# State-space stage: residuals of B and C formed by TensorE, two copies on ScalarE, and new instruction lists

## What is computed

```python
x = resid * lax.rsqrt(jnp.mean(resid * resid, -1, keepdims=True) + EPS) * norm_w
skip = x @ skip_w.T
xe = x @ in_w.T                      # then a causal convolution of 4 taps over time
xs = silu(conv(xe) + conv_b)
delta = softplus(xs @ wd1.T @ wd2.T + wd2_b)
A = -exp(A_log)                      # 256 channels x 16 states
Bm, Cm = xs @ wb.T, xs @ wc.T        # 16 values each per position
h = exp(delta * A) * h + (delta * xs) * Bm      # a scan over 256 positions
y = sum over states of h * Cm
y = (y + xs * W_D) * silu(skip)
out = resid + y @ out_w.T
```

## Time and profile before

| | us |
|---|---|
| median of 3 runs | 2874.43 |
| lowest, highest | 2872.92, 2874.45 |
| the profiled execution | 2875.4 |
| its span | 2873.6 |
| state-space stage, START to the end of MF | 0 to about 637 |

### The profile page before, as it was taken

The page is one execution under the profiler, slowest core; times in us unless marked ns, Lnnn a source line. Parts: engine busy times, 40 slices in busy tenths (PEclk is TensorE's granted clock), DMA queues, the critical chain, the costliest instruction groups (busy, mean ns, idle before and its releaser), DMA issues. The chain is left out here.

```text
span 2873.6 us, 55943 instructions
## 1 busy us (share of the span) xinstructions
PE 2647.1 (92%) x18868; PEld 1819.6 (63%) x18868; DVE 2260.1 (79%) x3798; ACT 2225.5 (77%) x6114; POOL 1223.4 (43%) x1089
## 2 busy tenths in 40 slices
PE   6888888789999999999999999997899999999997
PEld 3454445356666666666777777774566666666665
DVE  8999999976767777777689999996667777676774
ACT  5788878557777777777799999995677777777775
POOL 5776777664444444444400000001444444444442
PEclk8999999999999999999999999997999999999998
DMA  3000000000000000000000000000000000000000
GB/s 98 1 1 1 1 1 1 0 1 2 1 1 1 13 13 1 1 1 1 13 14 2 2 2 1 2 1 1 1 2 1 1 2 13 17 5 7 7 7 7
DMA packets 15672, 17.84 MB, mean 6 GB/s; under 512 B 3838, under 2 KB 12863, under 8 KB 15295
## 3 DMA queue, kind: packets, MB, share of 16 engines
q1 hardware_dynamic: 15390, 14.26, 1.7%
HBM read 12.16 MB, written 2.10 MB: 5 GB/s over the span
## 5 line engine op out<-in xcount | busy, mean ns | idle before, releaser
L1064 POOL TENSOR_TENSOR f_p<-f_p,f_rs 128x512 f32<-128x512 f32 (+1 forms) x256 | 321.2, 1255 | 907.4 <-DVE f_rs L1013 907.3
L901 ACT ACTIVATE f_p<-pair,f_nm 128x128 f32<-128x128 f32 (+1 forms) x1024 | 387.4, 392 | 125.2 <-DVE f_nm L1002 125.2
L679 POOL TENSOR_TENSOR m_hc<-m_h,m_c 128x512 f32<-128x512 f32 x256 | 323.4, 1284 | 154.5 <-DVE m_h L646 120.5
L1056 POOL TENSOR_TENSOR f_qb<-f_kn,f_tab 128x512 f32<-128x512 f32 x256 | 373.5, 1480 | 24.3 <-DVE f_kn L981 21.0
L646 DVE TENSOR_TENSOR_SCAN m_h<-m_a,pair 128x1024 f32<-128x1024 f32 x128 | 292.2, 2283 | 11.6 <-ACT m_a L608 1.9
L767 PE MATMUL pair<-f_wqkv,f_hT 128*128 128x512 f32 x512 | 248.7, 609 | 18.0 <-DVE f_kn L981 14.5
L608 ACT ACTIVATE m_a<-m_delta,m_A 128x255 f32<-128x255 f32 x512 | 217.3, 496 | 59.4 <-DVE m_h L646 58.8
L533 PE MATMUL bank<-m_hc,ident 128*128 128x512 f32 x512 | 248.2, 619 | 1.4 <-DVE X L655 1.3
L815 PE MATMUL pair<-ident,f_p 128*128 128x128 f32 x1536 | 244.7, 282 | 3.7 <-DVE f_pT L1007 2.4
L855 PE MATMUL bank<-f_hnT,f_w 128*128 128x256 f32 (+1 forms) x768 | 213.4, 401 | 12.5 <-ACT f_g L933 3.1
L815 PEld LDWEIGHTS pair<-ident,f_p 128*128 128x128 f32 x1536 | 170.6, 141 | 82.2 <-issue 60.0
(11 more groups left out here) (181 smaller groups left out, 6159.2 us busy)
## 6 DMA issues: line engine op xcount, KB each, us to landing
f_wqkv<-in_f_wqkv SPq DMA_DIRECT2D x4, 768.0 KB, 4.0
out_x<-X SPq DMA_DIRECT2D x16, 128.0 KB, 1.8
f_w<-in_f_w SPq DMA_DIRECT2D x4, 341.0 KB, 3.3
f_wo<-in_f_wo SPq DMA_DIRECT2D x4, 256.0 KB, 2.7
sel<-in_sel SPq DMA_DIRECT2D x1, 768.0 KB
f_w<-in_f_w SPq DMA_DIRECT2D x4, 192.0 KB, 3.2
m_taps<-in_m_taps SPq DMA_DIRECT2D x1, 512.0 KB, 3.6
X<-in_x SPq DMA_DIRECT2D x1, 512.0 KB, 8.5
```

What stands on the lines that cost most here:

```text
L679: op = nc.gpsimd.tensor_tensor(m_hc[:, g % 4, n], m_h[:, g % 2, n], m_c[:, g % 2, n].unsqueeze(1).broadcast_to([P, EC, L]), ALU.mult)
L901: op = nc.scalar.activation(f_p[:, t, j, k0:k1], SC[:, j, k0:k1], ACT.Exp, bias=f_nm[:, t, j:j + 1], accum_out=f_sm[:, t, j:j + 1])
L1056: op = nc.gpsimd.tensor_tensor(f_qb[:, t, :, o].rearrange("p (x h) d -> p x h d", x=2), f_kn[:, t, :, 32 - 32 * e:64 - 32 * e].rearrange(" ...
L1064: op = nc.gpsimd.tensor_tensor(f_p[:, t, :, k0:k1], f_p[:, t, :, k0:k1], f_rs[:, t, :].unsqueeze(2).broadcast_to([P, 4, k1 - k0]), ALU.mult)
```

## The change

1. `r1` and `mid` go, and with them the tiles `m_r` and `m_mid`. After `hi`, a new PE step `rh` multiplies the high part with minus the identity (`m_neg`, bf16) and accumulates it onto `m_bc_ps`, which then holds the residual. `mid2` copies that from PSUM. PE step `rm` takes the middle part off in the same way, and `lo`, now on ACT, copies what is left to the low part.
2. `ue` moves from DVE to ACT.
3. `xT` and the `bB`, `bC` steps wait for `lo` on ACT instead of DVE.
4. The four lists of `M_ORDER`, all of `START` and all of `MF` are written anew. In DVE's window `yg` stands behind `h1`, `x` ahead of `h3`, `delta` behind `h6`. In ACT's, `a4 c3 a5 c4` stand between `xs` and `gate`.
5. A setup step `neg` (two DVE instructions) makes `m_neg`. A gap in the memory layout is smaller by 368 elements.

```diff
@@ M_ORDER
-    "dve": "bx1 h1 bx2 yg h2 bx3 h3 ue bx4 x h4 bx5 h5 r1 bx6 delta h6 lo bx7 h7 bx0 h0",
-    "pe": "bB7 bB0 y4 bB1 bC0 y5 y6 bC1 y7 bB2 xT bC2 bB3 xe bC3 skip bB4 u bB5 out bc bC4 z bC5 y0 bB6 y1 bC6 y2 y3 "
-        "bC7",
-    "act": "xTe sq c2 a3 xs c3 gate a4 c4 a5 abs c5 exp hi ln a6 mid2 a7 c6 mid a0 c7 a1 c0 xr a2 c1",
-    "pool": "dx hc6 xx hc7 me rr hc0 hc1 hc2 hc3 hc4 hc5"}
+    "dve": "bx1 h1 yg bx2 h2 bx3 x h3 bx4 h4 bx5 h5 bx6 h6 delta bx7 h7 bx0 h0",
+    "pe": "bB7 y4 bB0 bC0 y5 bC1 bB1 y6 y7 xT bB2 bC2 bB3 xe out bB4 bC3 skip y0 bB5 u bC4 bB6 y1 bC5 bc bC6 z rh y2 "
+        "y3 bC7 rm",
+    "act": "xTe c2 sq a3 xs a4 c3 a5 c4 gate ue c5 hi a6 abs c6 exp mid2 ln lo a7 c7 c0 a0 a1 c1 xr a2",
+    "pool": "hc6 dx me hc7 rr hc0 hc1 hc2 hc3 xx hc4 hc5"}
...
+            elif s == "rh" or s == "rm":
+                if i == 1:
+                    pe.wait_ge(m_set, 6)
+                pe.wait_ge(*act_m.at(i, "hi" if s == "rh" else "mid2"))
+                r = slice(64, 96) if s == "rh" else slice(32, 64)
+                mm = nc.tensor.matmul(m_bc_ps, m_neg[r, :], m_bc[r, b, :], start=False, stop=s == "rm",
+                                      skip_group_check=True)
...
+            elif s == "ue":
+                act.wait_ge(*pe_m.at(i - 1, "z"))
+                act.wait_ge(*pe_m.at(i, "u"))
+                op = nc.scalar.activation(m_u[0:DD], m_u_ps, ACT.Copy)
             elif s == "mid2":
-                act.wait_ge(*dve_m.at(i, "r1"))
-                op = nc.scalar.activation(m_bc[32:64, b], m_r[64:96], ACT.Copy)
-            elif s == "mid":
-                act.wait_ge(*dve_m.at(i - 1, "lo"))
-                op = nc.scalar.activation(m_mid[64:96], m_r[64:96], ACT.Copy)
+                act.wait_ge(*pe_m.at(i, "rh"))
+                op = nc.scalar.activation(m_bc[32:64, b], m_bc_ps, ACT.Copy)
+            elif s == "lo":
+                act.wait_ge(*pe_m.at(i, "rm"))
+                op = nc.scalar.activation(m_bc[0:32, b], m_bc_ps, ACT.Copy)
...
-            if s == "ue":
-                dve.wait_ge(*pe_m.at(i, "u"))
-                dve.wait_ge(*pe_m.at(i - 1, "z"))
-                op = nc.vector.tensor_copy(m_u[0:DD], m_u_ps)
-            elif s == "r1":
-                dve.wait_ge(*act_m.at(i, "hi"))
-                dve.wait_ge(*act_m.at(i - 1, "mid"))
-                op = nc.vector.tensor_tensor(m_r[64:96], m_bc_ps, m_bc[64:96, b], ALU.subtract)
-            elif s == "lo":
-                dve.wait_ge(*act_m.at(i, "mid2"))
-                dve.wait_ge(*act_m.at(i, "mid"))
-                op = nc.vector.tensor_tensor(m_bc[0:32, b], m_r[64:96], m_mid[64:96], ALU.subtract)
...
@@ START, DVE: setup and the first sequence's steps
-    "dve": "n1: st mv z n2: st c0: nw inc n3: st n4: st n2: mv n3: mv n2: z n4: mv n5: st n6: st n7: st n8: st n5: "
+    "dve": "n1: st mv z n2: st n3: st n4: st c0: nw inc skip A n2: mv n3: mv n2: z n5: st n4: mv n5: mv c0: ones n6: "
...
@@ MF, DVE: around the last scan
-        "h4 bx5 n3: mv m17: h5 n5: st n4: mv n5: mv m17: bx6 f1: hT m17: h6 n6: st m17: bx7 f1: ss0 cl0 n7: st n8: "
-        "st f1: kn0 m17: h7 f1: qa0 ss1 cl1 qs0 kn1 qa1 n9: st n10: st n6: mv m18: yg n7: mv f1: qs1 n11: st m18: x "
+        "m17: bx4 n5: st m17: h4 bx5 h5 bx6 f1: hT m17: h6 n4: mv n5: mv m17: bx7 n2: z f1: ss0 cl0 m17: h7 f1: kn0 "
+        "n6: st f1: qa0 n7: st n8: st f1: ss1 cl1 qs0 kn1 n6: mv f1: qa1 n7: mv n8: mv n3: z m18: yg f1: qs1 n9: st "
```

More of the change, by code:

```diff
@@ L375, in build @@
         m_rr = m_sb("m_rr", [P, T])
-        m_r = m_sb("m_r", [96, L])
-        m_mid = m_sb("m_mid", [96, L], BF16)
+        m_neg = m_sb("m_neg", [96, 32], BF16)
         m_skip = m_sb("m_skip", [P, EC, P])
@@ L410, in build @@
         f_rs = m_sb("f_rs", [P, T, 4])
-        m_sb("f_gap", [P, 7520])
+        m_sb("f_gap", [P, 7152])
         f_sq = m_sb("f_sq", [P, 2 * INNER])
@@ L487, in m_pe @@
                 pe.wait_ge(*act_m.at(i, "xr"))
-                pe.wait_ge(*dve_m.at(i - 1, "lo"))
+                pe.wait_ge(*act_m.at(i - 1, "lo"))
                 for t in range(T):
@@ L512, in m_pe @@
                 for c in range(EC):
-                    mm = nc.tensor.matmul(o, w[:, c, :], m_xs[:, b, c, :], start=c == 0, stop=c == EC - 1)
+                    mm = nc.tensor.matmul(o, w[:, c, :], m_xs[:, b, c, :], start=c == 0, stop=s == "u" and c == EC - 1,
+                                          skip_group_check=True)
[5 more added lines that the diff above has]
+                mm = nc.tensor.matmul(m_bc_ps, m_neg[r, :], m_bc[r, b, :], start=False, stop=s == "rm",
+                                      skip_group_check=True)
             elif s == "z":
@@ L516, in m_pe @@
                     pe.wait_ge(m_set, 5)
-                pe.wait_ge(*dve_m.at(i, "ue"))
+                pe.wait_ge(*act_m.at(i, "ue"))
                 pe.wait_ge(*act_m.at(i, "gate"))
@@ L521, in m_pe @@
             elif k == "bB" or k == "bC":
-                pe.wait_ge(*dve_m.at(i, "lo"))
+                pe.wait_ge(*act_m.at(i, "lo"))
                 pe.wait_ge(*(m_before(dve_m, i, "bx", g, 2) if k == "bB" else m_before(act_m, i, "c", g, 1)))
@@ L617, in m_dve @@
             k, g = s.rstrip("0123456789"), int("0" + s[len(s.rstrip("0123456789")):])
-            if s == "ue":
-                dve.wait_ge(*pe_m.at(i, "u"))
-                dve.wait_ge(*pe_m.at(i - 1, "z"))
-                op = nc.vector.tensor_copy(m_u[0:DD], m_u_ps)
-            elif s == "r1":
-                dve.wait_ge(*act_m.at(i, "hi"))
-                dve.wait_ge(*act_m.at(i - 1, "mid"))
-                op = nc.vector.tensor_tensor(m_r[64:96], m_bc_ps, m_bc[64:96, b], ALU.subtract)
-            elif s == "lo":
-                dve.wait_ge(*act_m.at(i, "mid2"))
-                dve.wait_ge(*act_m.at(i, "mid"))
-                op = nc.vector.tensor_tensor(m_bc[0:32, b], m_r[64:96], m_mid[64:96], ALU.subtract)
-            elif s == "delta":
+            if s == "delta":
                 dve.wait_ge(*act_m.at(i, "ln"))
@@ L748, in f_pe @@
                     pe.wait_ge(*dve_m.at(NSEQ, "delta"))
+                    pe.wait_ge(*act_m.at(NSEQ, "lo"))
                 if i == 2 * NSEQ + 1:
@@ L1425, in first @@
                     op = nc.vector.tensor_scalar(m_A[:], m_A[:], -1.0, None, ALU.mult)
+                elif s == "neg":
+                    for r in (32, 64):
+                        op = nc.vector.tensor_scalar(m_neg[r:r + 32, :], ident[r:r + 32, r:r + 32], -1.0, None, ALU.mult)
                 elif s == "ones":
```

## The result

| | before | after |
|---|---|---|
| median, us | 2874.18 (4 runs, 2872.92 to 2874.45) | 2893.10 (4 runs, 2891.79 to 2897.35) |
| ratio, with its 95% interval | | 1.0069 [1.0056, 1.0083] |
| span of the profiled execution | 2873.6 | 2890.3 |

The prediction was 2872.2. The change costs 18.9 us by the medians and 16.7 by the spans. Every median here is over executions in the fast state; one of ten of the run e7_oldstart took 8476 us in the slow state and is left out.

What follows compares the result with a forecast made beforehand. The prediction took the state-space stage to be bound by DVE's list; 13 windows x (32.0 - 32.15) = -1.9 us, START -0.3 and MF 0 brought the median from 2874.43 to 2872.2, with an 8-in-10 range of 2862 to 2882.

Steps and rivals of the forecast that it cites:

- DVE's saving: Each state-space window: ue, r1 and lo leaving DVE save 0.09 + 0.35 + 0.33, rounded up to 0.8 us.
- the waits: DVE's waits already in each window of the kernel before, some for ACT's exponentials, taken as 0.1 us of 32.15.
- The chain from h3 to h7: Within a window, end of h3 to start of h7: DVE needs 13.3 us, ACT's chain 13.5, residual ready at 11.8.
- The lateness of 0.75: h7 late each window: 0.15 from ACT's chain plus 0.6 that lo waits for rm, making 31.25 into 32.0.
- The table loads: a4 and a5 between xs and gate add two ACT loads a window, 2 x 1.30 = 2.6 us.
- a rival: TensorE's clock falls after PE's wait before bC6: half speed adds 1.9 us every second window, 2884 us; chance 0.14.
- the falls of before: PE's clock drops behind gaps in the trace before, 0.65 in one stretch, read as delaying nobody.
- the forecast's own 32.0: Forecast window: 31.25 of DVE plus 0.75 lateness, against 32.15 before; windows of 31.8 to 32.2 had chance 0.45.
- START and MF: Joins around the windows: START -0.3 us (bounds -2.5 and +2), MF 0 (bounds -2.5 and +2.5); losing more: chance 0.07.

Runs made afterwards that it cites:

- e7_oldstart: Changed kernel with gate directly behind xs, and in START DVE's and POOL's lists of before without r1, ue, lo: 2867.84 us, ratio 0.9977 to before.

## Why the prediction was wrong

**DVE's saving** held: 31.07 to 31.10 a window with all waits gone, 1.06 to 1.08 less than before. ue, r1, lo were put at 0.8 and the waits at 0.1. The waits were 0.15 (five windows of twelve at 32.3 to 32.4, the others at 32.00), which leaves 0.90 to 0.93 for the three instructions. The price of a removed instruction was read well by the start-to-start steps.

**The chain from h3 to h7** held almost to the digit. `c5` ends 294.10 - 287.74 = 6.4 us behind the end of `h3` (6.5 forecast), `rm` starts in the window that keeps its length at 233.89, 11.7 behind it and 12.0 with its end (11.8), and `lo` waits there 0.79 (0.6). The lateness of 0.75 came as 0.45 at `bx7` and 0.45 at `h7`. `bB7`, which the prediction let pass as within 0.2 of its time, was the first of the two. That the window without a fall of the clock came to 31.98 for 32.0 is in part luck: DVE's own part was 0.17 too high and the lateness 0.15 too low.

**The table loads** are added as read, four a window, and cost 0.05 where the rest leaves room.

**The failing step** is the clock's: the sum has no term for PE's new wait ahead of `bC6`, and the runs show 13 x 1.25 = 16 us there (33.23 against 31.98), which go when the wait is filled. The mechanism, its place and its price for one window were written down, as a rival: a wait of about 2 us (measured 1.69), then half speed on `y2` and `y3`, +1.9 (measured 33.6 - 32.0, 1.6 to 1.7). Three things about it were off. It was given 0.14, with the falls of before read as delaying nobody, while DVE's waits of 0.33 behind five of them stand in the trace of before. It was priced for every second window, and falls in nine of twelve. And it was said to use up the gain of the windows from 0.6 us on; against the forecast's own 32.0, which is 0.15 under before, 0.15 is enough. With the rival's own numbers the kernel takes 2884, with the measured ones 2872.2 + 16 = 2888; the range ended at 2882.

**START and MF** came within their bounds of 2 and 2.5: +0.65 and about +2, where -0.3 and 0 were taken. They add 3 of the 20.9 us by which the median was missed, and the clock 16. The last 2 are the medians': the forecast put its median 1.0 under the profiled execution, as before, and it came 1.0 above (2893.10 and 2892.08).

## What to carry to other kernels

A new wait of PE can have two prices, its own length and half speed for what stands right behind it. Where a change puts such a wait ahead of a chain that others wait for, look in the profile before for a stretch with a like gap, see what the granted clock does behind it and which engine waits later for it, and give it a term in the sum. In how many windows it will fall was not to be read there: six of 13 before, nine of twelve after. Fill such a gap with work that has no wait (here one product moved, 2893 to 2864), before looking for anything dearer. And try new arithmetic on the old lists first: the best kernel here has the change's instructions and before's order.

## What the runs showed of the hardware

- PE's granted clock fell to 0.50, the level of 1.2 GHz, in nine of twelve windows behind a wait of 1.69 us, and in none behind one of 0.83 in the same place. In the other three windows a wait of the same 1.69 left it at 1.00, so the wait alone doesn't tell for one window.
- Before, the clock fell six times in 13 windows, and behind five of these falls DVE waited 0.18 to 0.34 us some 20 us later (followed in one window: through `xT`, `xs`, `gate` and `a4`).
- Added PE work made the kernel faster: 1.7 us of repeated products a window, 18.4 us less in all.
- A kernel whose clock is 0.50 for some 3 us in nine windows of twelve shows 0.96 as its mean against 0.98: the mean of a long stretch hides it, stretches of 2 us show it.
- Two table loads more in each window, 33 us of ACT in all, cost 0.7 us (13 x 0.05) where no engine waited for what they delay.
